# Row scatters that wait for units of the shared expert, shared units between the last attention groups, and the first routed block turned last

## What is computed

```python
x = x + jnp.tanh(g_xattn[0]) * _L0_xattn_ref(_layernorm(x), ctx_2048, ...)   # 16 heads, quantized
x = x + jnp.tanh(g_ffn[0]) * _L0_ffn_ref(_layernorm(x), ...)                 # 32 experts, 8 per token, and a shared one
x = x + jnp.tanh(g_xattn[1]) * _L1_xattn_ref(_layernorm(x), ctx_2048, ctx_2048)
x = x + jnp.tanh(g_ffn[1]) * _L1_ffn_ref(_layernorm(x), ...)                 # 32 experts, 6 per token, and a shared one
# an expert:  h = silu(x @ wg.T) * (x @ wu.T);  acc + cw[:, None] * (h @ wd.T)
```

## Time and profile before

| | us |
|---|---|
| median of 3 runs (lowest, highest) | 956.62 (956.19, 958.54) |
| the profiled execution | 963.2 |
| its span, first to last instruction | 961.5 |
| PE busy in the span | 744.2 (77%) |
| POOL busy | 480.6 (50%) |
| layer 0 attention, last exponential ends | 291.3 |
| first routed `gate_up` of layer 0 | 370.1 |
| first routed `gate_up` of layer 1 | 792.1 |

### The profile page before, as it was taken

How to read it: one execution, slowest core, us unless ns; L and a number is a source line. 1 busy time by engine, 2 the same in 40 slices (tenths; PEclk the granted TensorE clock), 3 DMA queues, 4 the chain that set the end, 5 groups by cost and what they waited for, 6 DMA issues and landing times.

```text
span 961.5 us, 20209 instructions
## 1 busy us (share of the span) xinstructions
PE 744.2 (77%) x5678; PEld 551.8 (57%) x5719; DVE 530.8 (55%) x1323; ACT 439.1 (46%) x1058; POOL 480.6 (50%) x530
## 2 busy tenths in 40 slices
PE   7657686777773759999999999368656389999965
PEld 4625454445543647777777777245444267777744
DVE  5989879778690524444444444377544044444424
ACT  3578676666662103444444444156531015555540
POOL 4726665888885631433333333391534704555540
PEclk9779867757655979999999999759875689999986
DMA  8919989999999834566665664674118325555536
GB/s 291 341 36 170 168 146 197 202 199 225 183 178 305 312 120 119 178 192 200 189 197 185 197 196 157 240 277 157 69 56 191 131 70 164 167 165 175 161 128 270
DMA packets 222101, 175.53 MB, mean 183 GB/s; under 512 B 146714, under 2 KB 200938, under 8 KB 220970
## 3 DMA queue, kind: packets, MB, share of 16 engines
q1 hardware_dynamic: 207994, 132.52, 54.4%
q0 software_dynamic: 13728, 41.17, 11.8%
q10 hardware_dynamic: 272, 0.52, 0.2%
HBM read 87.92 MB, written 52.69 MB: 146 GB/s over the span
## 4 chain that ended last, share of the span: by engine, by line
PE 47%; DVE 10%; DMA 9%; issue 8%; POOL 8%; another core or an unknown queue 7%; ACT 5%; SPq 1%; POOLq 0%; DVEq 0%; ACTq 0%
PE psum L974 16%; PE psum L1007 13%; DMA pT<-p 6%; PE psum L986 4%; POOL p L1671 3%; PE psum L940 3%; PE psum L962 3%; ACT e L1147 3%; DVE nmax L1291 3%; POOL y_dram L1694 2%; DMA W<-y_dram 2%; PE psum L835 2%; DMA y_dram<-ybuf,idxi 1%; PE psum L1063 1%
## 5 line engine op out<-in xcount | busy, mean ns | idle before, releaser
L1694 POOL DMA_INDIRECT y_dram<-ybuf,idxi x174 | 167.3, 962 | 257.5 <-ACT ybuf L1196 200.9
L1470 DVE COPY hT<-psum 88x256 f32<-88x256 f32 (+2 forms) x214 | 74.3, 347 | 245.5 <-issue 88.4
L974 PE MATMUL psum<-W,xTs 128*128 x696 | 192.9, 400 | 0.6 <-issue 0.6
L1147 ACT ACTIVATE e<-psum,nmax 128x1024 f32<-128x1024 f32 x128 | 142.6, 1114 | 67.9 <-POOL p L1671 39.1
L1291 DVE TENSOR_REDUCE nmax<-psum 128x1 f32<-128x1024 f32 x128 | 152.8, 1218 | 35.1 <-PE psum L835 23.0
L1671 POOL TENSOR_SCALAR p<-e 128x1024 f16<-128x1024 f32 x128 | 133.9, 1046 | 65.9 <-ACT e L1147 39.3
L1186 ACT ACTIVATE sg<-psum 128x176 f32<-128x176 f32 (+2 forms) x214 | 61.2, 286 | 181.3 <-PE psum L974 77.5
L1196 ACT ACTIVATE ybuf<-psum,dot 128x256 f32<-128x256 f32 x174 | 82.5, 474 | 106.7 <-PE psum L1007 94.5
L1684 POOL DMA_INDIRECT xs_dram<-xaug,posi x112 | 110.1, 983 | 37.5 <-issue 33.1
L974 PEld LDWEIGHTS psum<-W,xTs 128*128 128x128 f32 x696 | 114.1, 190 | 21.8 <-issue 1.6
L835 PE MATMUL psum<-kstack,qstack 128*128 128x512 bf16 x215 | 91.4, 502 | 43.0 <-ACT e L1147 34.5
(11 more groups left out here) (223 smaller groups left out, 1152.8 us busy)
## 6 DMA issues: line engine op xcount, KB each, us to landing
xs<-xs_dram SPq DMA_DIRECT2D x174, 160.0 KB
W<-in_wffn SPq DMA_DIRECT2D x15, 1024.0 KB, 13.4
xs_dram<-zeros SPq DMA_DIRECT2D x2, 5120.0 KB, 26.1
oT<-in_wffn SPq DMA_DIRECT2D x96, 88.0 KB
osb_v<-in_wffn SPq DMA_DIRECT2D x94, 88.0 KB
W<-y_dram SPq DMA_DIRECT2D x6, 1024.0 KB, 6.6
W<-y_dram SPq DMA_DIRECT2D x8, 768.0 KB, 9.1
W<-in_wffn SPq DMA_DIRECT2D x4, 768.0 KB
```

The lines of the kernel that those rows point to most:

```text
L974: last = pe.matmul(out, xTs[:, n % 2, k, :], Wv[layer][:, k, :, :, bass.DynSlice(of_block[q][0], 1), :], start=k == 0, stop=k == KD - 1)
L1147: act.activation(e[:, s % 2, :], bank(s_bank(s), 2), ACT.Exp, bias=nmax[:, s % S_RING:s % S_RING + 1], accum_out=esum[:, t, head:head + 1] ...
L1694: pool.indirect_dma_start(y_dram[layer][:, :], bass.IndirectOffsetOnAxis(idxi[:, slot:slot + 1], 0), ybuf[:, b % Y_RING, :], None).then_in ...
```

## The change

Four edits, on all engines but SP:

- **Gates.** In layer 0 the scatters 34 to 47 (counted from 0) each wait for one more `silu` of shared units (the first for one), and 48 to 55 for 16 to 23 of them; 56 to 63 wait for nothing new. The layer norm of pair 3 moves from before scatter 42 to before scatter 40. In layer 1 the scatters 30 to 45 each wait for one more of that layer's 16 shared units.
- **Shared units in the tail.** PE does the steps 0 and 1 of `ffn` behind the first two of the last four `attend`.
- **Pair 3 later.** Its chain moves three steps back (two for `o_transposed`), on PE, ACT and DVE alike; DVE's `tile_out(7)` goes from before step 0 to step 2.
- **First block last.** Where the last shared unit stands, PE turns the first routed block behind `gate_up`, `h_transposed` and `down`, and ACT copies it behind `silu`.

```diff
-                    if q + 1 < end and routed(q + 1):
+                    if q + 1 < end and routed(q + 1) and routed(q):
                         x_block_transposed(q + 1)
...
+                    if q + 1 < end and routed(q + 1) and not routed(q):
+                        x_block_transposed(q + 1)
+                        expert_in(q + 1)
...
                     if s >= LAG:
                         attend(s - LAG)
-
-                o_transposed(3)
-                for i in range(LAST[0] - FIRST[0] + 2):
-                    if i == 1:
+                    if s == STEPS:
+                        pe.wait_ge(c2["exp"], STEPS)
+                    if s in (STEPS, STEPS + 1):
+                        ffn(0, s - STEPS)
+
+                for i in range(2, LAST[0] - FIRST[0] + 2):
+                    if i == 3:
+                        o_transposed(3)
+                    elif i == 4:
                         project(3)
-                    elif i == 4:
+                    elif i == 7:
                         x_transposed(0, 3)
-                    elif i == 5:
+                    elif i == 8:
                         route(0, 3)
-                    elif i == 6:
+                    elif i == 9:
                         rank(0, 3)
-                    elif i == 9:
+                    elif i == 12:
                         spread(0)
                     ffn(0, i)
...
-                while sent < 42:
-                    scatter(0, sent)
-                    sent += 1
-                norm_rstd(pool, step, 6, 3, cn[0]["stats"], cn[0]["rstd"])
-                while sent < NT * TOP[0]:
-                    scatter(0, sent)
-                    sent += 1
+                for j in range(sent, NT * TOP[0]):
+                    if j == 40:
+                        norm_rstd(pool, step, 6, 3, cn[0]["stats"], cn[0]["rstd"])
+                    if j < 48:
+                        pool.wait_ge(cf["s"], j - sent + 1)
+                    elif j < 56:
+                        pool.wait_ge(cf["s"], j - 48 + 16)
+                    scatter(0, j)
...
                 for i in range(NT * TOP[1]):
+                    if 30 <= i < 46:
+                        pool.wait_ge(cf["s"], FIRST[1] + i - 29)
                     scatter(1, i)
```

## The result

The changed kernel takes 947.19 us (median of 4 runs, 945.23 to 948.49) where the kernel before takes 956.4 in the same session (954.63 to 958.54): ratio 0.9907 [0.9882, 0.9932], 9.2 us less. A second measurement, on another chip beside the experiments, gave 953.81 against 966.3: 0.9856 [0.9809, 0.9904]. The forecast was 949.0, in 940 to 960.

A forecast was written before the change was run, and what follows sets the result against it. PE bounds most stages, so each layer's routed start counts, delayed by PE stalls beside unbroken POOL scatters. Gains of 5.1 us (layer 0) and 2.5 (layer 1) sum to 7.6: 956.6 - 7.6 = 949.0 us, range 940 to 960.

The forecast's parts named there:

- The idle at 299 to 307: Layer 0, behind the last attend: PE would go on at 298.7 instead of 307.3, with tile_out at about 299.
- Units and tail in layer 0: Layer 0's gated shared units end with silu(22) at 344.8; eight more scatters follow, and gate_up(24) comes at 362.4.
- PE idle for 14 us: Before layer 0's routed units PE would idle 14 to 17 us, and about 10 before layer 1's.
- Layer 1's first units: Layer 1's shared units: gate_up(4) at 755.3 (before 759.15), gate_up(5) at 758.5 (before 774.36).
- layer 0's term: Layer 0's routed stage would stand as if it began at 365.0, not 370.1: a gain of 5.1 us.
- half clock: PE resumes after idle at about half its clock; charged 2.6 us at layer 0's routed start, 2.4 at layer 1's.
- margin: Layer 0: some 17 us between SP's first block issue and PE reaching that block, which the gates spend.
- layer 1's term: Layer 1's routed start at 787.2, with half clock 789.6, against 792.1: a gain of 2.5 us.
- The delay comes back at the gates' pace: Rival: each gated scatter holds back PE's increment, so gates open later; at 1.0 us a unit 967 us; chance 0.14.
- The idle is cheaper than I charge: Rival: no delay at the units' pace and no clock loss at the routed starts: 941.3 us; chance 0.23.
- The gates don't bind: Rival: POOL lags the units, gates are already open, only 1 to 3 us gained: 955; within the 0.19 for same.
- The stalls are something else's: Rival: engines wait for their code, gates remove nothing, tails add 17 us in layer 0, 12 in layer 1: 986; chance 0.03.

The follow-up runs named there:

- no_gates1: The changed kernel without layer 1's gates: 962.14 us, ratio 0.9979 to the kernel before.
- mid_l1: The kernel before with a POOL memset of 128x320 behind each scatter in layer 1 alone: 945.26 us, ratio 0.9805.
- before_small: The kernel before with a POOL memset of 128x2 behind layer 0's scatters from the 35th and all of layer 1's: 956.54 us, ratio 0.9899.
- no_gates0: The changed kernel without layer 0's gates: 955.11 us, ratio 0.9893 to the kernel before.
- fill64: The kernel before with a POOL memset of 128x64 behind layer 0's scatters from the 35th and all of layer 1's: 943.83 us, ratio 0.9802.
- after_fill: The changed kernel without gates, with a 128x128 memset behind layer 0's scatters from the 35th and all of layer 1's: 938.99 us, ratio 0.9737.
- best: The kernel before with a 128x128 memset behind layer 0's scatters from the 35th and layer 1's first 38: 934.82 us, ratio 0.9703.
- before_mid: The kernel before with a POOL memset of 128x320 behind layer 0's scatters from the 35th and all of layer 1's: 938.62 us, ratio 0.9698.
- no_tail: The changed kernel with shared units 0 and 1 behind the last attend, not between the last four: 955.94 us, ratio 0.9922.
- warm0: The changed kernel with 14 unused matmuls on PE behind layer 0's last shared unit, to fill the idle time: 954.31 us, ratio 0.9879.
- early0: The changed kernel with other gates in layer 0 that leave no scatter behind the last unit: 942.91 us, ratio 0.9746.

## Why the prediction was right, and where not

The time came out 1.8 us under the forecast, and the mechanism is the one it named. That the sum of 7.6 us came so near was luck: its two terms were both off, in opposite directions.

**Right.** *The idle at 299 to 307*: PE is busy 8.20 of 8.30 us, `tile_out` starts at 300.4 for "near 299". *Units and tail in layer 0*: `silu(22)` at 343.4 (forecast 344.8), the last scatter at 354.0 (355.2), `gate_up(24)` at 361.2 (362.4). The chain between the two took the 7.2 us that were costed, but of other parts: SP came 2.7 us behind the last scatter (4.1 costed), the landing took 2.3 (2.3), and turn and copy 2.2 (0.8), since PE turns the second block too ahead of `gate_up(24)` and waited 1.05 us for it. *The wait that the gates put before pair 3's layer norm*: 2.2 us before `x_transposed` (2.0). *PE idle for 14 us* before layer 0's routed units, and 7.8 (forecast 10) before layer 1's. *Layer 1's first units*: with layer 0's lead of 2.9 us added back, `gate_up(5)` stands at 758.3 (758.5).

**Wrong: layer 0's term, 5.1 us forecast, 3.8 and 1.0 measured.** The timed runs of `no_gates1` put it, together with block 0's later turn, at 1.9 us. The start itself was right: `gate_up(24)` comes 9.8 and 8.3 us earlier than before, counted from the last exponential, and the first routed `silu` 8.6 and 7.1, where 370.1 - 362.4 = 7.7 was forecast. The half clock cost what was charged, as far as the rows show it: 1.2 us from `gate_up(24)` to its `silu` and 1.5 and 1.2 at the next unit, for 2.6. What failed is the step "In this idle time y-scatters and SP's loads queue behind the last scatter, as before", which charged nothing else behind the start. Up to the seventh routed `silu` the lead shrinks by 3.0 and 5.0 us against before, and by 1.9 and 1.0 more until the stage ends. In the first profile about 1.5 us of the 3.0 is the second unit at half clock (3.44 us from `silu` to `silu` for 1.95), and 1.5 the wait of `goes_to` for the eighth block (3.96 for 2.49); in the second 1.2 and 3.8. In the earlier trace rows SP's 20 us head start was visible, and I used it as "margin" that the gates may spend. It wasn't idle margin: it was what kept blocks ahead of PE. The traces of all kernels bear that out; SP's lead is from its first block to `gate_up(24)`, in us:

```
SP's lead     kernels                                     clock at gate_up(24)   fifth to sixth routed silu
16.2 to 20.0  before, mid_l1, before_small, no_gates0     1.00                   2.49
9.6           fill64                                      1.00                   2.49
8.4           after_fill                                  1.00                   2.55
7.8           best                                        1.00                   3.40
6.0           before_mid                                  0.50                   6.38
4.4 to 4.6    the changed kernel twice, no_gates1,        0.50                   3.96 to 6.71
              no_tail, warm0, early0
```

That it is the loads and not the clock shows in `best`: its clock is 1.00 from 325 us to the end of layer 0's routed units, and DVE waits for a block all the same:

```profile
367.00 0.45 DVE L1484 TENSOR_TENSOR both<-xs,own 128x256 f32<-128x256 f32 x1 [3.27 <-DMA xs<-xs_dram]
```

At one and the same lead the wait still differs by up to 2.8 us; what sets its length I don't know.

**Wrong: layer 1's term, 2.5 us forecast, 8.1 measured in shared 1.** The two numbers count different things: the 2.5 are a start 792.1 - 787.2 = 4.9 us earlier, less 2.4 for the half clock behind it. Counted from the first shared `silu`, the first routed `gate_up` comes 9.0 us earlier, so the start was under-forecast by 4.1. Most of that, 3.0 us, is the stretch from `gate_up(5)` to `silu(15)`: 15.7 us (755.4 to 771.1) where 16.15 + 1.2 + 1.4 = 18.75 was forecast. Of the 1.4 charged as delay at the gates' pace (11 x 0.13) only 0.4 came. And the 16.15 were taken from a stretch of the earlier trace rows that began at half clock, so they were some 2.0 too long. The rest is smaller: `gate_up(5)` 0.7 earlier, `silu(15)` to the last scatter 0.5 longer, from there to `gate_up` 6.4 for 7.2. The charge of 2.4 for the half clock is not shown to be wrong: 0.8 us of it lies ahead of the first routed `silu`, and from there to the eleventh the changed kernel takes 16.3 and 18.0 us in its two profiles where the kernel before takes 16.3, so 0.8 in one and 2.5 in the other. The four other kernels with gates in layer 1 take 17.6 to 18.4 there, the four that start at granted clock 1.00 (before, `no_gates1`, `before_small`, `fill64`) 16.3 to 17.0.

**The rivals.** *The delay comes back at the gates' pace* fell: some 0.04 us a unit. Its sum for the upper end of the range was off too: 0.9 us a unit in one layer alone gives some 957 us, not 960. Its bound from above was layer 1's routed stage with a scatter every 1.73 us; the open paces now show units at PE's own 1.41 us beside scatters 1.62 us apart, so that row bounded nothing of this kind. *The idle is cheaper than I charge* was half right: the delay was next to nothing, but in layer 0 the idle cost more. *The gates don't bind* fell with the 1.41 us of the timeline. *The stalls are something else's*: with the open pace of 1.62 us the same code, and 78 instructions more, runs without a stall, and the stalls grow with the scatters' rate alone. Nor does a load of code end them: in the kernel before no packet of an instruction queue lies between 742 and 786 us, where both of layer 1's stalls begin and end, and the two beside layer 0's stalls lie at 301.0 and 338.2 (the second just ahead of the window of the earlier trace rows), 5.8 and 8.7 us before those end. The rule cited from the Trainium skill, "Runtime: NRT & Kernel Launch", section "Instruction fetch mechanics", that an engine's code comes in 16 KiB blocks over a DMA queue of its own, is borne out as the cause of these stalls by no run here.

**What I left out.** The prediction took the run of scatters as the unit of harm and looked at the shared units only. The scatters beside layer 1's attention cost more than those beside either layer's shared units: 14.4 of its 133.0 us go with the pace of 1.62, and the change doesn't touch them.

## What to carry to other kernels

Where one engine's increments arrive late beside a run of indirect scatters, set the scatters' pace before writing gates: one instruction of 0.4 us behind each gave 27.7 us, where gates, tail and order by hand gave 9.2 and 12.5. A gate works too, and at a shorter distance, but it reaches only the stretch for which it was written. And a wait that moves an issuing queue's start next to its consumer's spends a lead that the consumer lived on: before calling such a distance margin, look at what the queue does a few blocks later.

## What the runs showed of the hardware

**How late PE's increments come depends on the scatters' distance, by degrees.** Longest distance of two shared units in layer 1 (ACT's `silu`), beside a queue of scatters that runs by itself: scatters 1.27 us apart, 16.9 us; 1.36, 12.8; 1.41, 4.4; 1.46, 3.4; 1.62, 2.4, and from the fifth unit to the fifteenth 1.41, which is PE's own time (the last unit is left out: at 1.62 it waits 23.5 us for the first routed block, which comes behind the last scatter). With each scatter gated on the unit's `silu`, most distances are 1.41, but in each gated kernel one of 2.2 to 2.4 is among them.

**Held increments came on a beat.** In `best` from 740 to 749 PE's increments, by the semaphore events of the trace, arrive about 1.45 us apart (743.03, 744.51, 745.97, 747.42, 748.86), and a unit that needs two of them takes 2.9; in `fill64` three, 4.35. The beat stays 1.45 until 750.3, though the scatters' distance in `best` goes from 1.46 to 1.27 at 744.2; then it breaks up. A reading that fits, and that no run tests: a scatter takes some 1.45 us of something that the increments need too, so that at less than that a queue builds up, at 1.62 it drains, and behind a gate none can form. At 1.27 and 1.36, however, increments come far more rarely than on that beat (in the kernel before, four between 745 and 772), so it is not the whole of it. Which path they share, the traces don't say, and I leave it open.

**A clock that fell behind 2.2 us of idle.** In `warm0` PE worked at the full level, granted clock 1.00, until 356.9, and had 0.50, the lower level, in 361 to 366, after a wait of 2.2 us and blocks that came singly; behind it stands 0.99 in 366 to 368.
